# A metaformer with routed experts: tiles kept per half, expert buffers in the first half's memory, new instruction lists

## The chip, the cores and the metric

The kernel runs on one core of a Trainium2 chip. The time is that of the device, in microseconds, from the first to the last instruction of the program and a little around it; a figure for a kernel is the median of its runs. The core has five engines that work through lists of their own: TensorE (PE, with its weight loads shown apart as PEld), VectorE (DVE), ScalarE (ACT), GpSimd (POOL) and SyncE (SP, which issues most DMAs here). They wait for one another by semaphores.

## The reference

`x` holds 2 batches of 16 times by 64 patches, with 128 channels. It is normalised per position, goes through four layers of attention, and is added to its own input; then comes a layer of eight experts of which each token takes two.

```python
b, t, p, d = x.shape
for i in range(DEPTH):                                # 4 layers, 8 heads of 16
    xs = _layernorm(x.reshape(b * t, p, d), ln_s_g[i], ln_s_b[i])
    x_s = _attention(xs, w_qkv_s[i], w_out_s[i], b_out_s[i]).reshape(b, t, p, d)   # over 64 patches
    xt = (x + x_s).transpose(0, 2, 1, 3).reshape(b * p, t, d)
    xt = _layernorm(xt, ln_t_g[i], ln_t_b[i])
    x_t = _attention(xt, w_qkv_t[i], w_out_t[i], b_out_t[i])                       # over 16 times
    x_t = x_t.reshape(b, p, t, d).transpose(0, 2, 1, 3)
    x = _layernorm(x_s + x_t, ln_f_g[i], ln_f_b[i]) + x
```

```python
probs = jax.nn.softmax(xf @ Wr, axis=-1)
w, idx = jax.lax.top_k(probs, 2)
gates = jnp.zeros((n, e)).at[jnp.arange(n)[:, None], idx].add(w)
acc = acc + g[:, None] * (gelu(xf @ w1) @ w2)         # summed over the 8 experts, and added to x
```

## The kernel before

**Halves and units.** The two batches are the two halves of the work, 1024 tokens or 8 chunks of 128 each. A word such as `score.t10` names a step: `t` for temporal (`s` spatial, `e` the experts, `f` the layer's last norm), the half (1), and the group (0). Spatial attention of a half has two groups, temporal attention one unit. A minus behind the word means the layer before, a plus the next one.

**Steps of a layer.** DVE computes the moments (`stats`) and POOL the root (`stats` too, a power, line 499); DVE normalises four chunks and ACT the other four (`normal`); PE transposes them (`turn`). PE makes keys and queries (`project`, line 748) and values (`values`, line 727), DVE and POOL apply the rotation, and PE folds the keys' two parts into one (`fold`, lines 758 and 760). PE computes scores in two halves of four heads, `score` and `more` (line 795; temporal ones start from a mask, line 787). DVE takes the maximum off and ACT the exponential, first half `soft`, second half `rest`. PE transposes the probabilities (`head`, `tail`) and multiplies them with the values (`lead`, `mix`, line 832), DVE divides (`divide`), PE applies the output weights (`out`, line 868), and DVE adds the residual (`out`). `bias` and part of the last norm (`final`) prepare the next layer's sum. A matmul of float32 shows twice in the profile's counts.

**Glows.** A step `glow` is four matmuls of `ident` by `ident` into a bank of `turn` that no instruction reads (line 695).

**Experts.** For each half, PE computes the logits, DVE picks two experts per token (`rank`) and then the slot of each pair (`place`, which needs a small matmul of PE on `chosen`). POOL sends each token to its two slots by 16 indirect DMAs (`send`, line 540, two to a step), SP loads the slots back in four parts (line 468) once all 16 have landed, and DVE reads gates and owners from them (`origin`). Then 46 blocks of 128 slots are run: in tick i PE computes the first product of block i and the second of block i-1, DVE copies the first weights of block i+1 (`w1_now`, line 967) and scales the result of block i-1 (`y_sb`), and POOL sends that result back by an indirect DMA (line 549). At the end DVE adds the two answers to each token (`merge`).

**Order.** Each engine runs its steps strictly in order, and nothing but lists sets that order: `ORDERS` (line 102) for layers 0 to 2 and `TAIL` (line 130) for layer 3 and the experts, one list for each of PE, DVE, ACT and POOL. In `TAIL` the number behind `@` says ahead of which tick a step stands. Between them the list of PE in a layer reads, around the temporal score pairs of both halves:

```python
score.s11 more.s11 head.s10 lead.s10 tail.s10 mix.s10 score.t00 more.t00 head.s11 lead.s11 tail.s11 mix.s11 glow.s02 out.s10 glow.s07 glow.s01 glow.s03
head.t00 lead.t00 tail.t00 mix.t00 turn.t10 project.t10 out.t00 fold.t10 score.t10 more.t10 values.t10 glow.s04 turn.s00+ glow.s00
```

**Memory.** `x_res`, `x_bias`, `x_mid`, `x_sum` and `x_nrm` are one tile each for both halves. `qT`, `kE`, `v_s` and `prob` lie in an arena whose memory the experts' buffers (`slots0`, `slots1`, `xT`, `w1_now`, `hT`, `y_sb`) take over when attention is done with it.

## Time and profile before

| | us |
|---|---|
| median of three runs | 669.15 |
| lowest and highest run | 665.67, 670.98 |
| time of the profiled execution | 671.71 |
| its span in the trace | 669.9 |
| PE busy | 550.3 |
| DVE busy | 454.9 |
| ACT busy | 305.9 |
| POOL busy | 249.0 |

The profile covers one execution. Busy times count the instructions of an engine without its waits; a row of a timeline gives the start, the time, the engine, the line, the operation, what it writes and reads, how many instructions were merged into the row, and in brackets how long the engine had been idle and what released it. The granted clock of PE is given as a share of full speed: 1.00 is 2.4 GHz and 0.50 is 1.2 GHz.

### The profile page before, as it was taken

What the parts mean: (1) busy time and instruction counts of PE and PEld (TensorE: products, weight loads), DVE (VectorE), ACT (ScalarE), POOL (GpSimd) and SP (SyncE); (2) the same over time, 40 slices, a digit from 0 to 9 for tenths busy, and PEclk for the clock granted to TensorE, in tenths of its full rate; (3) what the DMA queues carried; (4) which work ended last, traced back from release to release, by engine and by line L of the source; (5) the groups of instructions that cost most, each with busy time, mean ns of one, the idle gap of its engine ahead of it and who ended that gap; (6) DMA issues with size and microseconds to landing.
All of it is one profiled execution on the core that took longest, in us unless ns stands there. A gap on an engine that the chain in (4) does not pass through costs nothing.

```text
span 669.9 us, 21398 instructions
## 1 busy us (share of the span) xinstructions
PE 550.3 (82%) x8984; PEld 432.4 (65%) x8984; DVE 454.9 (68%) x1336; ACT 305.9 (46%) x507; POOL 249.0 (37%) x197
## 2 busy tenths in 40 slices
PE   0978988897898977978988798889888736999991
PEld 0565676566756846665677467746766635999991
DVE  5586847948877576788755966986479676444444
ACT  1455833274466433744844256448434313343330
POOL 6403501441253031613700424154014273777642
PEclk9999979799999897989979979999798575999996
DMA  4000008400000100000001000000000014141314
GB/s 134 1 2 1 3 3 298 174 2 18 1 3 4 32 1 4 2 18 1 2 4 33 2 2 3 17 1 3 3 2 3 6 46 110 50 145 53 107 38 141
DMA packets 17425, 24.71 MB, mean 37 GB/s; under 512 B 2578, under 2 KB 12180, under 8 KB 17268
## 3 DMA queue, kind: packets, MB, share of 16 engines
q1 hardware_dynamic: 14836, 18.17, 8.7%
q0 software_dynamic: 2496, 5.18, 2.3%
q8 instruction: 73, 1.20, 0.8%
q14 instruction: 20, 0.16, 0.1%
...
## 4 chain that ended last, share of the span: by engine, by line
PE 63%; DVE 15%; ACT 11%; issue 5%; POOL 2%; DMA 2%; SPq 0%; DVEq 0%; ACTq 0%
PE turn L678 8%; PE small L832 8%; PE score L748 7%; PE score L795 7%; PE small L933 6%; PE score L921 6%; PE small L727 5%; PE turn L695 4%; PE turn L758 4%; PE turn L760 3%; DVE stats L955 3%; ACT probT L626 3%; PE small L868 3%; ACT prob L620 2%; ACT kE L613 2%
## 5 line engine op out<-in xcount | busy, mean ns | idle before, releaser
L499 POOL TENSOR_TENSOR rstd<-veps,mhalf 128x8 f32<-128x8 f32 x28 | 46.5, 1661 | 246.1 <-DVE veps L995 246.1
L626 ACT ACTIVATE probT<-turn 128x512 f32<-128x512 f32 x96 | 53.3, 597 | 94.9 <-PE turn L678 94.7
L1088 DVE TENSOR_REDUCE top<-score 128x16 f32<-128x1024 f32 (+1 forms) x48 | 58.5, 1219 | 39.2 <-PE score L795 39.2
L795 PE MATMUL score<-kE,qT 32*32 32x64 f32 (+1 forms) x3072 | 58.6, 261 | 12.2 <-issue 12.1
L795 PEld LDWEIGHTS score<-kE,qT 32*32 32x32 f32 (+1 forms) x3072 | 48.8, 123 | 27.1 <-issue 26.0
L678 PE MATMUL turn<-ident,prob 128*128 128x128 f32 x384 | 61.2, 311 | 2.9 <-ACT prob L620 2.9
L1090 DVE TENSOR_TENSOR prob<-score,top 128x1024 f32<-128x1024 f32 x48 | 58.8, 1224 | 1.6
L678 PEld LDWEIGHTS turn<-ident,prob 128*128 128x128 f32 x384 | 49.2, 160 | 6.7 <-ACT prob L620 3.6
L549 POOL DMA_INDIRECT answers<-y_sb,home x46 | 44.7, 971 | 23.9 <-DVE y_sb L1224 16.5
L832 PE MATMUL small<-v_s,probT 128*64 128x34 f32 x1024 | 43.0, 240 | 12.5 <-ACT probT L626 6.8
L620 ACT ACTIVATE prob<-prob 128x1024 f32<-128x1024 f32 x48 | 50.1, 1057 | 6.9 <-DVE prob L1090 6.7
L613 ACT ACTIVATE kE<-turn,hmask 128x512 f32<-128x512 f32 x64 | 39.9, 686 | 28.3 <-PE turn L760 28.1
L832 PEld LDWEIGHTS small<-v_s,probT 128*64 128x64 f32 x1024 | 39.0, 153 | 21.0 <-ACT probT L626 8.7
L921 PE MATMUL score<-xT,w_now 128*128 128x128 f32 x368 | 50.5, 282 | 1.2 <-ACT xT L657 0.9
L933 PE MATMUL small<-w_all,hT 128*128 x368 | 48.8, 276 | 0.0
L664 ACT ACTIVATE hT<-score 128x512 f32<-128x512 f32 x46 | 27.5, 597 | 46.1 <-PE score L921 46.1
L921 PEld LDWEIGHTS score<-xT,w_now 128*128 128x128 f32 x368 | 46.3, 198 | 2.0 <-issue 1.3
L604 ACT ACTIVATE v_t<-small 32x512 f32<-32x512 f32 x64 | 38.8, 607 | 17.2 <-PE small L727 16.5
L1058 DVE TENSOR_TENSOR rope<-score,cs_t 128x512 f32<-128x512 f32 x48 | 30.7, 681 | 23.5 <-PE score L748 23.5
L933 PEld LDWEIGHTS small<-w_all,hT 128*128 128x128 f32 x368 | 44.8, 192 | 0.2
L540 POOL DMA_INDIRECT dispatched<-routed,slot_idx x32 | 32.4, 1012 | 32.9 <-DVE slot_idx L1187 23.8
L695 PE MATMUL turn<-ident 128*128 128x128 f32 x280 | 40.0, 293 | 2.9 <-ACT xnT L589 1.5
...
## 6 DMA issues: line engine op xcount, KB each, us to landing
...
```

The lines of the kernel that those rows point to most:

```text
L613: last = nc.scalar.activation(kE[:, e, cols], turn[:, u % 2, :], ACT.Copy, scale=hmask[:, e:e + 1])
L620: nc.scalar.activation(p, p, ACT.Exp, scale=SCALE).then_inc(prob_ready, 1)
L626: nc.scalar.activation(probT[:, q.nth % 2, 2 * k:2 * k + 2, 2 * h:2 * h + 2, :].rearrange("p k g n -> p k (g n)"), turn[:, u % 2, :].rearr ...
L678: last = nc.tensor.transpose(turn[:, u % 2, j * P:(j + 1) * P], src, ident[:, :])
L695: nc.tensor.matmul(turn[:, q.turns % 2, 0:P], ident[:, :], ident[:, :], start=True, stop=True)
L748: nc.tensor.matmul(score[:, i % 4, :], w[:, off:off + P], cols, start=True, stop=True).then_inc(proj_full, 1)
L795: last = nc.tensor.matmul(score[b * n:(b + 1) * n, g, c * 2 * n:(c + 1) * 2 * n], qT[rows, tok:tok + n], kE[rows, :, tok:tok + n], start=q ...
L832: last = nc.tensor.matmul(cols[b * n:(b + 1) * n, :, g, :], probT[:, head.nth % 2, k, g, b * n:(b + 1) * n], v[:, blk0 + b, g, :], start=T ...
L921: last = nc.tensor.matmul(score[:, i % 4, c * P:(c + 1) * P], w1_now[:, i % WAYS, c * P:(c + 1) * P], xT[:, g % 2, b % XGROUP * P:(b % XGR ...
L933: last = nc.tensor.matmul(bank[:, 0:P], hT[:, j % 2, c * P:(c + 1) * P], w2_all[:, bass.ds(e, 1), c * P:(c + 1) * P].rearrange("p o n -> p ...
L1088: nc.vector.tensor_reduce(tops, mine, AX_X, ALU.max).then_inc(top_ready, 1)
L1090: nc.vector.tensor_tensor(prob[:, i % 2, 2 * h:2 * h + 2, :, :].rearrange("p g k (r n) -> p (g k r) n", n=block_len), mine, tops[:, :, Non ...
```

## The change

**Tiles.** `x_nrm`, `x_mid`, `x_bias`, `x_sum`, `x_res`, `qT` and `kE` become two tiles each, one for each half, all within the arena. `slots0`, `xT`, `w1_now` and `hT` move into what the first half's tiles held, `slots1` to the arena's start, `y_sb` into the memory of `kE` of the first half. All uses are rewritten to the half's own tile, with the same shapes.

**Lists.** All eight lists are new. On PE, steps are woven more finely: in a layer `tail.s10`, `head.s11` and `mix.s10` stand between `score.t00` and `more.t00`, and two glows between `score.t10` and `more.t10`; a layer has eight glows before and after, and the last layer with the ticks five instead of eleven. In `TAIL`, ticks 0 to 2 stand ahead of the second half's `place.e10` on PE and DVE, and the second half's sends are spread over ticks 1 to 8 on POOL. On DVE, `normal.e00` moves ahead of `rank.e00`, and `divide.s11` between `soft.t00` and `rest.t00`; on POOL, `stats.f10` stands behind six `send` steps of the first half instead of five.

```diff
-ARENA = (53760 + 16384) // 4
+HALF = 6 * HT * 4
+ARENA = (20480 + 2 * HALF + 16384 + 8704 + 16384 + 768) // 4
...
-        score.s11 more.s11 head.s10 lead.s10 tail.s10 mix.s10 score.t00 more.t00 head.s11 lead.s11 tail.s11 mix.s11 glow.s02 out.s10 glow.s07 glow.s01 glow.s03
+        score.s11 more.s11 head.s10 lead.s10 score.t00 tail.s10 head.s11 mix.s10 more.t00 tail.s11 lead.s11
...
-        origin.e00@0 place.e10@0 origin.e10@21 merge.e00@47 merge.e10@47
+        origin.e00@1 place.e10@3 origin.e10@24 merge.e00@47 merge.e10@47
...
-        qT = at("qT", [P, TOKENS], 20480)
-        kE = at("kE", [P, 2, TOKENS], 28672)
...
+        def halves(name, slot):
+            return [at(f"{name}{h}", [P, HC, P], 20480 + h * HALF + slot * HT * 4) for h in range(BATCH)]
+
+        x_nrm, x_mid, x_bias, x_sum, x_res = (halves(name, i) for i, name in enumerate(("x_nrm", "x_mid", "x_bias", "x_sum", "x_res")))
+        qT = [at(f"qT{h}", [P, HT], 20480 + h * HALF + 5 * HT * 4) for h in range(BATCH)]
+        keys = 20480 + 2 * HALF
+        kE = [at(f"kE{h}", [P, 2, HT], keys + h * 8192) for h in range(BATCH)]
...
-        hT = at("hT", [P, 2, FF], 24576)
-        slots1 = at("slots1", [P, BLOCKS, ROW], 28672)
-        y_sb = at("y_sb", [P, ANSWERS, P], 17664)
-        w1_now = at("w1_now", [P, WAYS, FF], 40832)
...
+        slots0 = at("slots0", [P, BLOCKS, ROW], 20480)
+        xT = at("xT", [P, 2, XGROUP * P], 20480 + 12160)
+        w1_now = at("w1_now", [P, WAYS, FF], 20480 + 12160 + 4096)
+        hT = at("hT", [P, 2, FF], 20480 + 12160 + 8192)
+        y_sb = at("y_sb", [P, ANSWERS, P], keys)
+        slots1 = at("slots1", [P, BLOCKS, ROW], 0)
```

**PE, from the first half's temporal scores to out.s10, in a layer.** Before, the two score halves (each a mask and 64 matmuls on `kE` and `qT`) stand together, and glows (`turn<-ident`) around `out.s10` (`o_nrm` and the 128x128 matmuls on `xnT`):

```order
L787 MATMUL score<-pmask 128x512 x2
L795 MATMUL score<-kE,qT 32x64 x64
L787 MATMUL score<-pmask 128x512 x2
L795 MATMUL score<-kE,qT 32x64 x64
L678 MATMUL turn<-ident,prob 128x128 x8
L832 MATMUL small<-v_s,probT 64x34 x16
L678 MATMUL turn<-ident,prob 128x128 x8
L832 MATMUL small<-v_s,probT 64x34 x16
L695 MATMUL turn<-ident 128x128 x4
L678 MATMUL turn<-ident,o_nrm 128x128 x8
L868 MATMUL small<-ws,xnT 128x128 x8
L695 MATMUL turn<-ident 128x128 x12
```

In the changed kernel the same place reads:

```order
L791 MATMUL score<-pmask 128x512 x2
L799 MATMUL score<-kE_64,qT_62 32x64 x64
L685 MATMUL turn<-ident,prob 128x128 x16
L836 MATMUL small<-v_s,probT 64x34 x16
L791 MATMUL score<-pmask 128x512 x2
L799 MATMUL score<-kE_64,qT_62 32x64 x64
L685 MATMUL turn<-ident,prob 128x128 x8
L836 MATMUL small<-v_s,probT 64x34 x32
L685 MATMUL turn<-ident,o_nrm 128x128 x8
L872 MATMUL small<-ws,xnT 128x128 x8
L685 MATMUL turn<-ident,prob 128x128 x16
L702 MATMUL turn<-ident 128x128 x8
```

Sixteen transposes and 16 matmuls on `probT` have moved between the two score halves, no glow stands next to `out.s10`, and two glows (8 matmuls) stand behind the transposes of `head.t00` and `tail.t00`.

**PE, the second half's temporal scores, in a layer.** Before, the folds, the two score halves, the values, a glow, and the next layer's `turn.s00` between two glows:

```order
L758 MATMUL turn<-rope_49,ident 128x512
L760 MATMUL turn<-rope_50,exch 128x512
L787 MATMUL score<-pmask 128x512 x2
L795 MATMUL score<-kE,qT 32x64 x64
L787 MATMUL score<-pmask 128x512 x2
L795 MATMUL score<-kE,qT 32x64 x64
L727 MATMUL small<-wt,xnT 32x64 x64
L695 MATMUL turn<-ident 128x128 x4
L678 MATMUL turn<-ident,x_nrm 128x128 x8
L695 MATMUL turn<-ident 128x128 x4
```

In the changed kernel:

```order
L731 MATMUL small<-wt,xnT 32x64 x64
L762 MATMUL turn<-rope_49,ident 128x512
L764 MATMUL turn<-rope_50,exch 128x512
L762 MATMUL turn<-rope_49,ident 128x512
L764 MATMUL turn<-rope_50,exch 128x512
L791 MATMUL score<-pmask 128x512 x2
L799 MATMUL score<-kE_65,qT_63 32x64 x64
L702 MATMUL turn<-ident 128x128 x8
L791 MATMUL score<-pmask 128x512 x2
L799 MATMUL score<-kE_65,qT_63 32x64 x64
L685 MATMUL turn<-ident,x_nrm_52 128x128 x8
```

The values have moved ahead of the folds, and two glows stand between the score halves and none behind them.

**DVE, the second half's `place.e10` and the first blocks.** Before, the end of `place.e10` (down to `code_of`) stands ahead of the copies of tick 1 and 2 (a load of the expert's number, then `w_now<-w_all`) and of the scaling of block 0 (`y_sb`):

```order
L1191 TENSOR_TENSOR reach<-small_60,rc 128x184
L1193 TENSOR_REDUCE picked<-reach 128x23
L1194 TENSOR_SCALAR expert_of<-picked 128x23
L1196 TENSOR_SCALAR code_of<-picked 128x23
L966 TENSOR_LOAD expert_of
L966 ISA x2
L967 ISA
L967 COPY w_now<-w_all 128x512
L1224 TENSOR_SCALAR y_sb<-small,gate 128x128
L966 TENSOR_LOAD expert_of
```

In the changed kernel the end of `origin.e00` (`home`), ticks 1 and 2, and then the start of `place.e10`:

```order
L1210 SCALAR_TENSOR_TENSOR home<-slots_78,picked 128x23
L970 TENSOR_LOAD expert_of
L970 ISA x2
L971 ISA
L971 COPY w_now<-w_all 128x512
L1223 TENSOR_SCALAR y_sb<-small,gate 128x128
L970 TENSOR_LOAD expert_of
L970 ISA x2
L971 ISA
L971 COPY w_now<-w_all 128x512
L1223 TENSOR_SCALAR y_sb<-small,gate 128x128
L1171 TENSOR_SCALAR small_68<-small 128x8
```

Two copies and two scalings, those for blocks 2 and 3 and of blocks 0 and 1, now stand ahead of `place.e10`.

## Rows read from the trace of the kernel before

**Rows 1.** The page, busy time: us, share of the span, instructions of one engine.

```profile
PE 550.3 (82%) x8984; PEld 432.4 (65%) x8984; DVE 454.9 (68%) x1336; ACT 305.9 (46%) x507; POOL 249.0 (37%) x197
```

**Rows 2.** The page, the chain that ended last: shares of the span by engine.

```profile
PE 63%; DVE 15%; ACT 11%; issue 5%; POOL 2%; DMA 2%; SPq 0%; DVEq 0%; ACTq 0%
```

**Rows 3.** Stages: stretch, length, busy (instructions) of PE, PEld, DVE, ACT, POOL; PE's granted clock; DMA.

```profile
148.30:275.50 127.20, 109.49 (x2028) 81.23 (x2024) 94.14 (x262) 65.57 (x109) 39.83 (x28) 0.93 0.03 8
...
511.50:558.90 47.40, 30.62 (x520) 26.50 (x516) 33.07 (x130) 13.57 (x24) 23.84 (x20) 0.65 0.08 25
571.40:656.40 85.00, 84.76 (x750) 84.12 (x750) 35.50 (x93) 32.58 (x55) 57.25 (x59) 1.00 0.25 79
```

**Rows 4.** Stages: six stretches at half clock (two, sum), one more, one at full clock.

```profile
214.80:221.60 6.80, 5.77 (x138) 4.96 (x133) 4.01 (x4) 2.14 (x3) 0.00 (x0) 0.50 0.01 2
255.80:262.50 6.70, 5.67 (x239) 4.90 (x237) 6.56 (x20) 1.65 (x4) 1.64 (x1) 0.50 0.02 5
...
sum 47.30, PE 41.12 PEld 34.32 DVE 33.58 ACT 12.88 POOL 4.91; mean PE 6.85 PEld 5.72 DVE 5.60 ACT 2.15 POOL 0.82
...
474.20:481.00 6.80, 6.61 (x117) 5.70 (x99) 2.73 (x3) 2.74 (x4) 0.00 (x0) 0.50 0.02 5
351.40:381.90 30.50, 25.02 (x367) 18.64 (x363) 22.31 (x81) 10.97 (x20) 8.39 (x6) 1.00 0.06 19
```

**Rows 5.** Timeline of PE around out.s10, layer 1: start, us, instructions, [idle before].

```profile
228.15 2.84 PE L695 MATMUL turn<-ident 128*128 128x128 f32 x24
...
232.38 0.86 PE L832 MATMUL small<-v_t,probT 128*32 128x68 f32 x32 [0.52 <-DVE x_sum L1002]
...
237.13 1.09 PE L678 MATMUL turn<-ident,x_nrm 128*128 128x128 f32 x8
```

**Rows 6.** Timeline of PE, layer 1, from more.t00 on.

```profile
216.50 1.11 PE L795 MATMUL score<-kE,qT 32*32 32x64 f32 x57 [1.03 <-issue]
...
219.44 1.95 PE L832 MATMUL small<-v_s,probT 128*64 128x34 f32 x32
...
222.78 1.17 PE L832 MATMUL small<-v_s,probT 128*64 128x34 f32 x32 [0.25 <-ACT probT L626]
```

**Rows 7.** Timeline of PE, layer 1: values.t00, then values.t10.

```profile
191.91 1.99 PE L727 MATMUL small<-wt,xnT 128*32 128x64 f32 x128
...
259.57 3.51 PE L727 MATMUL small<-wt,xnT 128*32 128x64 f32 x128
```

**Rows 8.** Timeline of DVE, layer 1: out.s10's first sum, normal.t10's products.

```profile
227.56 0.69 DVE L1116 TENSOR_TENSOR x_mid<-small,x_bias 128x512 f32<-128x512 f32 x1 [2.71 <-PE small L868]
...
233.38 1.11 DVE L1024 TENSOR_SCALAR x_nrm<-x_mid,mv,rstd 128x128 f32<-128x128 f32 x4
```

**Rows 9.** Timeline of PE, start of layer 2: lead.s00.

```profile
291.95 0.67 PE L832 MATMUL small<-v_s,probT 128*64 128x34 f32 x16 [1.47 <-DVE x_sum L1125]
```

**Rows 10.** Timeline of DVE: the first instruction of rank.e00.

```profile
524.33 0.22 DVE L1139 TENSOR_TENSOR marks<-small,rstd 128x64 f32<-128x64 f32 x1 [3.01 <-PE small L878]
```

**Rows 11.** Timeline of DVE: normal.e10's products; the weight copy for block 2.

```profile
563.75 1.11 DVE L1024 TENSOR_SCALAR routed<-x_in,mv,rstd 128x128 f32<-128x128 f32 x4
...
570.88 0.43 DVE L967 COPY w_now<-w_all 128x512 f32 x1 [0.76 <-DVE code_of L1196]
```

**Rows 12.** Timeline of POOL: the tenth send of the first half, then stats.f10.

```profile
545.06 0.96 POOL L540 DMA_INDIRECT dispatched<-routed,slot_idx  x1 [0.30 <-issue]
546.98 1.70 POOL L499 TENSOR_TENSOR rstd<-veps,mhalf 128x8 f32<-128x8 f32 x1 [0.96 <-DVE veps L995]
```

**Rows 13.** Timeline of PE: place.e10, block 4, the second half's first slots.

```profile
563.81 0.23 PE L887 MATMUL small<-chosen,tri 128*128 128x64 bf16 x1 [5.03 <-DVE chosen L1162]
...
575.12 1.06 PE L921 MATMUL score<-xT,w_now 128*128 128x128 f32 x8
...
607.37 0.60 PE L678 MATMUL turn<-ident,slots 128*128 128x128 f32 x4
```

**Rows 14.** Loads of the slots (line 468): from issue to landing.

```profile
DMA to landing us min/median/max: 3.3/5.2/6.9
```

150 lines of the change are left out of this document (69 added, 81 removed).

## The prediction

> **What bounds the kernel now.** I read the page's busy lines first, then the chain that ended last, then the busy times by stage, and only then single instructions. PE is busy for 82% of the span [rows 1]. The chain runs through PE for 63% and through DVE for 15% [rows 2], so PE's list decides, and DVE's where PE waits. By stage [rows 3]: layer 1, which stands for the three full layers, takes 127.2 us with PE busy 109.49 at a granted clock of 0.93; the stretch in which the two halves are routed takes 47.4 with PE busy only 30.62 at 0.65; the expert blocks take 85.0 with PE busy 84.76 at 1.00. In the blocks only PE's own speed counts. What new lists can change lies in the layers and in the 47.4 us of routing.
>
> Two things cost PE time in a layer. The first is the clock. In each of layers 0 to 2 there are two longer stretches at a granted 0.50, which is 1.2 GHz of 2.4: six in all, 47.3 us with PE busy 41.12, and a seventh in layer 3 of 6.8 with 6.61 busy [rows 4]. In each case PE had just run a pair of temporal score halves. In layer 1, score.t00 and more.t00 stand back to back, 128 matmuls each in the profile's count, and the clock falls at 214.8, within the second; behind score.t10 and more.t10 it falls at 255.8 [rows 4]. The second thing is the glows, matmuls of ident by ident that nobody reads: of the four that stand around out.s10 in PE's list, the three behind it take 2.84 us [rows 5].
>
> **The change part by part.** *Tiles per half and the arena.* The same instructions work on the same shapes; only addresses differ. I put that at nothing, and both bounds too: no row shows an operation that would change.
>
> *The clock at score pairs.* The new list puts tail.s10, head.s11 and mix.s10 between score.t00 and more.t00, and two glows between score.t10 and more.t10; in layer 3 the t00 pair is split too (by tail.s10 and mix.s10), the t10 pair is not. What a half-clock stretch costs: 32 narrow matmuls take 1.95 against 1.17 [rows 6], 128 value matmuls 3.51 against 1.99 [rows 7]. By the last pair the factor is 1.76, so the six stretches lose 41.12 x (1 - 1/1.76) = 17.8 and the seventh 6.61 x 0.432 = 2.9: together 20.6, some 2.9 each. PE is late all through these stretches, so nothing hides it. The bounds are 0 (the clock falls all the same) and 20.6 (it never does). The nearest row for a split pair is the stretch from 351.4 to 381.9, which kept 1.00 with PE busy 25.02 of 30.5 [rows 4]; the nearest against it is that in a pair PE has also an idle time of 1.03 that a split does not take away [rows 6]. Halfway between them I take half, 10.3.
>
> The Trainium skill, page "TensorE: Matmul & The Clock Gate", section "Part 4: PE-mode transpose", says that the full rate does not engage for transposes, which are not counted as busy in the same way. By that rule transposes between the two halves of a pair would hold nothing, and this term would be nearer 0. Here the trace speaks against it in part: from 219.44 to 222.78 PE ran only narrow matmuls and transposes, and the clock came back between them [rows 6].
>
> *The glows.* There are eight per layer before and after. Of the four around out.s10, one goes from ahead of out.s10 and three from ahead of head.t00; two stand now behind tail.t00, where PE would wait for x_sum anyway (0.52 before [rows 5]). What that gives is capped by DVE, which is late next: from out.s10's first sum at 227.56 to the end of normal.t10's products at 234.49 [rows 8], so turn.t10 could start at 234.5 where it starts at 237.13 [rows 5]: 2.6 at most. Against it stands a new wait: divide.s11 now stands between soft.t00 and rest.t00 on DVE, and out.s10 waits for what follows it. I take 2.0 per layer, bounds 0 and 2.6, over four layers 8.0. The other glows go into waits as they did. values.t10 moves from behind more.t10 to ahead of fold.t10: its 1.99 [rows 7] leaves one place of PE's path and enters another, nothing.
>
> *The start of a layer.* head.s01 and tail.s00 now fill the 1.47 that lead.s00 waits for x_sum [rows 9]; but lead.s01 then waits for divide.s00, which stands behind stats.f10 on DVE. Bounds 0 and 1.5 for each of three layers; nearer to nothing, since the wait is only moved, and I take nothing.
>
> *Routing of the first half.* normal.e00 moves ahead of rank.e00 on DVE, into 3.01 us in which DVE waits for the logits [rows 10]; its 1.1, by the 1.11 of normal.e10 [rows 11], leaves the path to the first send. But stats.f10's pow now stands behind 12 sends instead of 10, at 0.96 and 0.30 between two of them, 1.26 each, and DVE's final.f10 waits for it: before, POOL had been free for 0.96 when it was wanted [rows 12], so 2.5 - 0.96 = 1.5 comes back. Sum 0.4 lost; bounds 1.1 gained (the pow is hidden) and 1.5 lost. I take nothing.
>
> *Blocks ahead of the second half's routing.* PE waits 5.03 for chosen before place.e10 [rows 13]; blocks 0 to 2 now stand ahead of that. Yet blocks 2 and on need weight copies from DVE, and DVE works in order. Before, it begins normal.e10's products at 563.75, then does origin.e00 and place.e10 up to 570.12 (the copy for block 2 at 570.88, less the 0.76 ahead of it [rows 11]): 6.4. From there to PE's matmuls of block 4 at 575.12 [rows 13] it does three copies and two y_sb: 5.0. After, the same 6.4 + 5.0 stand between 563.75 and block 4, in another order: two copies and two y_sb between origin.e00 and place.e10. So PE's wait only moves, from ahead of block 0 to ahead of block 4. Bounds: 5.0 gained (the whole wait of PE) and 0.8 lost (one more such wait of 0.76 for PE's place.e10). I take nothing.
>
> *Second half's sends.* They begin when place.e10's indices stand, one copy (0.43 + 0.76) ahead of block 4's start after, so at some 574, and seven answers of the first blocks stand between them on POOL: 16 + 7 = 23 transfers of 1.26 [rows 12] are 29, so the last goes at 603 and the slots land 5.2 later [rows 14], at 608. PE wants the second half's first slots at 607.37 [rows 13], and a shift of all that went before moves both. Bounds 0 and 2 lost; I take nothing, since origin.e10 has been put three blocks later as well.
>
> **The sum.** 10.3 + 8.0 = 18.3. The profiled execution's span is 669.9 and its own time 671.71, so 1.8 lies around the span; 669.9 - 18.3 + 1.8 = 653.4. That execution was 2.6 above the median of the three runs, 669.15: I forecast 651 as a median.
>
> **The rivals.**
> 1. *The clock holds at all seven pairs.* For it: most of what PE did just ahead of each fall was the pair itself. Against: the 1.03 of idle time within the pair stays [rows 6]. 669.15 - 20.6 - 8.0 = 640.6.
> 2. *The clock falls as often.* For it: only transposes and narrow matmuls stand between the t00 halves. 669.15 - 8.0 = 661.2. This is also what the rule on transposes in the Trainium skill, named above, would make of t00.
> 3. *The glows were needed.* Without four of them between mix.s11 and mix.t00, PE runs only transposes and narrow matmuls there, and a new stretch at 0.50 appears in each of four layers: 4 x 2.9 = 11.6 is given back. 651 + 11.6 = 662.6.
> 4. *Slower.* From more.s11 to out.s10's full matmuls the new list has nothing but narrow matmuls and transposes: four sets of 8 transposes at 1.09 [rows 5], four of 32 narrow matmuls at 1.17 and two score halves of 128 x 1.11 / 57 / 1.76 = 1.4 [rows 6], some 12 us at full clock. If the clock stays at 0.50 there to the end, that costs 12 x 0.76 = 9.1 instead of 2.9, 25 more in four layers; less the 8.0 of glows the time is 669 + 17 = 686. It decides against the change when more than some 6.5 us of that work runs at half clock.
> 5. *The blocks do fill the wait.* DVE turns out not to bind, and blocks 0 to 2 fill the 5.03 of PE's wait [rows 13]: 5 more, 646.
>
> **How the numbers follow.** My forecast 0.37; rival 1 0.18; rival 2 0.20; rival 3 0.12; rival 4 0.08; rival 5 0.05. 1% is 6.7 us, about what a measurement of this kernel can tell from no change. Faster by over 1% (below 662.5): 0.37 + 0.18 + 0.05 + half of rival 2's and a little of rival 3's = 0.72. Slower: 0.09. The rest, 0.19, is within 1%. The range for 8 in 10 reaches from just below rival 1 to rival 2 with its own error: 638 to 667. The forecast's own range, with the clock terms between 6 and 15 and the glows between 0 and 10, is 644 to 663.
>
> **What would show it.** Clock: in the stage table of the new kernel, the stretches at 0.50 behind score.t00 or score.t10 should be about half as many as seven; every one kept costs 2.9. Glows: turn.t10 should wait for x_nrm of DVE, some 7 us behind out.s10's first sum. Blocks: PE should wait some 2 to 3 us for w_now ahead of block 4. Sends: a wait for the second half's slots of at most 2 us. The prediction is wrong if the layers do not shorten by some 4 to 6 us each, or if the stretch from the last score pair to block 4 changes by more than 3 us.

## The result: no change, at 669.33 us

The changed kernel took 669.33 us as a median of 20 runs (657.13 to 678.70), the kernel before 670.01 as a median of 20 (665.67 to 672.75). The forecast was 651, in a range of 638 to 667. The ratio that the comparison gives is 0.9909 (95% interval 0.9883 to 0.9935), but it leaves out every run more than 1.5% above its kernel's fastest, and the new kernel scatters so widely that this was more than half of its runs; medians over all runs are compared here, and by them nothing changed. The clock did not change either: the mean granted clock of an execution is 0.914 as a median of the 20 runs, and 0.917 over the 123 runs of the kernel before that stand beside the experiments. The profiled execution took 674.03, 4.7 above the median; its span is 672.1.

The page's busy time and chain of the changed kernel answer to [rows 1] and [rows 2]:

```profile
PE 556.5 (83%) x8936; PEld 433.6 (65%) x8936; DVE 454.9 (68%) x1336; ACT 307.3 (46%) x507; POOL 249.2 (37%) x197
...
PE 59%; DVE 21%; ACT 7%; issue 6%; POOL 4%; DMA 1%; DVEq 0%; SPq 0%; ACTq 0%; POOLq 0%
```

PE has 48 instructions less (six glows) and is busy 6.2 us longer: it ran more of its work at half clock. The chain goes through DVE for more of the span (21% against 15%). The stages, to be read beside [rows 3] (layer 1; the routing of both halves, with values.t10 in it now; the blocks, here from block 4 on, in [rows 3] from block 2 on):

```profile
152.30:281.40 129.10, 112.88 (x2028) 82.72 (x2024) 94.30 (x262) 65.92 (x109) 39.97 (x28) 0.92 0.03 8
512.90:561.10 48.20, 30.92 (x628) 26.91 (x628) 34.64 (x135) 14.41 (x25) 21.72 (x20) 0.65 0.11 34
576.40:658.70 82.30, 81.93 (x726) 81.25 (x726) 33.89 (x89) 30.92 (x52) 57.76 (x59) 1.00 0.26 82
```

Layer 1 is 1.9 longer in this execution, the routing 0.8 longer, and PE is still busy without a break in the blocks. The stretches at half clock that follow a temporal pair in layers 0 to 3 of this execution, beside [rows 4]:

```profile
86.70:100.30 13.60, 13.22 (x238) 10.94 (x239) 3.72 (x6) 5.25 (x8) 0.00 (x0) 0.50 0.01 2
131.10:144.70 13.60, 13.43 (x287) 10.11 (x287) 8.44 (x25) 5.38 (x10) 1.64 (x1) 0.50 0.02 5
216.40:219.80 3.40, 3.40 (x16) 2.85 (x15) 0.00 (x0) 2.20 (x4) 0.00 (x0) 0.50 0.02 5
260.80:274.40 13.60, 13.06 (x176) 9.06 (x176) 7.45 (x13) 6.54 (x12) 0.00 (x0) 0.50 0.01 2
387.10:400.70 13.60, 12.72 (x198) 9.14 (x198) 7.13 (x11) 5.82 (x10) 0.00 (x0) 0.50 0.01 2
472.40:486.00 13.60, 13.60 (x357) 11.69 (x337) 4.30 (x8) 4.28 (x6) 0.00 (x0) 0.50 0.02 4
sum 71.40, PE 69.44 PEld 53.79 DVE 31.04 ACT 29.47 POOL 1.64; mean PE 11.57 PEld 8.97 DVE 5.17 ACT 4.91 POOL 0.27
```

Before, seven stretches held 41.12 + 6.61 = 47.7 us of PE's work; now six hold 69.4. One pair kept the clock (layer 2's first), one lost it only shortly (layer 1's first), and the other five have stretches of 13.6. All three second pairs of layers 0 to 2 are among these. PE's timeline of the one in layer 0:

```profile
131.09 2.04 PE L799 MATMUL score<-kE,qT 32*32 32x64 f32 x128
133.07 3.78 PE L702 MATMUL turn<-ident 128*128 128x128 f32 x16
136.78 1.03 PE L791 MATMUL score<-pmask 2*128 2x512 bf16 x2
137.74 2.04 PE L799 MATMUL score<-kE,qT 32*32 32x64 f32 x128
139.72 1.97 PE L685 MATMUL turn<-ident,x_nrm 128*128 128x128 f32 x8
141.85 4.66 PE L752 MATMUL score<-xnT,ws 128*128 128x512 f32 x7 [0.17 <-ACT xnT L596]
```

The two glows between the halves take 3.78 us at half clock and do not bring it back; more.t10, turn.s00 and most of project.s00 run at half clock behind them. In this execution the split stretched the time at half clock instead of ending it. That is not the lists alone: in the kept execution of `e5_old_tail` (below), whose lists of layers 0 to 2 are the same, two of the three stretches behind the second pairs are short:

```profile
129.00:139.20 10.20, 9.54 (x151) 6.67 (x151) 5.23 (x10) 4.95 (x9) 0.79 (x1) 0.50 0.01 3
255.30:258.70 3.40, 3.40 (x31) 3.23 (x31) 2.83 (x5) 0.28 (x1) 0.00 (x0) 0.50 0.02 5
378.20:381.60 3.40, 3.40 (x52) 3.23 (x52) 2.56 (x4) 0.00 (x0) 0.00 (x0) 0.50 0.02 5
```

### The profile page after: what moved, and what is told of

It reads as the page before. It is cut to its first block, busy times and chain, and to the rows that moved or that the text cites. A ratio compares the mean times of both kernels' runs of the same rounds, so it can differ in the third digit from the quotient of the medians.

```text
span 672.1 us, 21303 instructions
## 1 busy us (share of the span) xinstructions
PE 556.5 (83%) x8936; PEld 433.6 (65%) x8936; DVE 454.9 (68%) x1336; ACT 307.3 (46%) x507; POOL 249.2 (37%) x197
## 4 chain that ended last, share of the span: by engine, by line
PE 59%; DVE 21%; ACT 7%; issue 6%; POOL 4%; DMA 1%; DVEq 0%; SPq 0%; ACTq 0%; POOLq 0%
PE turn L685 9%; PE score L799 7%; PE score L752 6%; PE small L937 6%; PE small L836 6%; PE score L925 6%; DVE stats L959 5%; PE turn L762 4%; PE turn L764 4%; PE small L731 4%; PE turn L702 3%; PE small L872 3%; POOL rstd L507 2%; ACT xnT L647 2%; DVE mv L990 2%
## 5 line engine op out<-in xcount | busy, mean ns | idle before, releaser
L799 PE MATMUL score<-kE,qT 32*32 32x64 f32 (+1 forms) x3072 | 62.9, 267 | 9.0 <-issue 8.5
L799 PEld LDWEIGHTS score<-kE,qT 32*32 32x32 f32 (+1 forms) x3072 | 51.7, 125 | 26.3 <-issue 22.5
L557 POOL DMA_INDIRECT answers<-y_sb,home x46 | 45.1, 980 | 20.6 <-DVE y_sb L1223 11.7
L1103 DVE RECIPROCAL den<-small 128x16 f32<-128x16 f32 x64 | 16.1, 252 | 48.8 <-PE small L836 48.3
L836 PE MATMUL small<-v_s,probT 128*64 128x34 f32 x1024 | 40.7, 240 | 6.9 <-DVE o_nrm L1105 4.2
L647 ACT ACTIVATE xnT<-turn 128x512 f32<-128x512 f32 x32 | 17.4, 594 | 58.5 <-PE turn L685 58.5
L518 POOL TENSOR_TENSOR rope<-rope,cs_s 128x512 f32<-128x512 f32 x16 | 20.3, 1270 | 62.3 <-DVE rope L1078 62.3
```

Source lines behind the costliest of these rows:

```text
L557: nc.gpsimd.indirect_dma_start(ys[h], bass.IndirectOffsetOnAxis(home[:, h, b % BLOCKS:b % BLOCKS + 1].bitcast(U32), 0), y_sb[:, b % ANSWER ...
L799: last = nc.tensor.matmul(score[b * n:(b + 1) * n, g, c * 2 * n:(c + 1) * 2 * n], qT[q.half][rows, tok:tok + n], kE[q.half][rows, :, tok:t ...
L836: last = nc.tensor.matmul(cols[b * n:(b + 1) * n, :, g, :], probT[:, head.nth % 2, k, g, b * n:(b + 1) * n], v[:, blk0 + b, g, :], start=T ...
```

## The experiments

Eighteen kernels ran in batches, each batch beside runs of the kernel before. The difference is between medians of one batch; 6 to 12 runs of each kernel stand behind a median, and their spread is mostly 5 to 12 us (19 in f4, 15 in j2, and one run of e5 took 804.99), so that two medians less than some 2 us apart are not told apart. Two kernels of different batches are compared by their differences to the kernel before; four medians stand behind such a figure, and below some 4 us it is not told from chance by itself. If the recorded runs are drawn again at random, 95 of 100 draws put f1 between 4.0 and 12.0 behind e5, but f3 anywhere from 6.8 ahead of e5 to 0.5 behind it. The last two columns give the mean granted clock, as the median over the same runs: it tells whether a difference in time is one of the clock. Ratios come with a 95% interval and leave out runs as said above.

| run | what it is | median | before beside it | difference | clock | clock before |
|---|---|---|---|---|---|---|
| (the change) | all of it | 669.33 | 670.01 | -0.7 | 0.914 | 0.917 |
| e6_tiles_only | new tiles, old lists | 669.37 | 668.66 | +0.7 | 0.915 | 0.917 |
| e4_old_layers | new list of layer 3 and experts alone | 672.70 | 668.66 | +4.0 | 0.906 | 0.917 |
| e5_old_tail | new lists of layers 0 to 2 alone | 665.35 | 668.66 | -3.3 | 0.927 | 0.917 |
| e1_join_both | the change, all split pairs joined again | 672.94 | 668.66 | +4.3 | 0.916 | 0.917 |
| f1_t00_joined | e5, first pair joined | 673.34 | 668.76 | +4.6 | 0.911 | 0.917 |
| f2_values_between | e5, values between the second pair | 665.55 | 668.76 | -3.2 | 0.926 | 0.917 |
| f3_glows_at_out | e5, glows at out.s10 | 663.03 | 668.76 | -5.7 | 0.930 | 0.917 |
| f4_tail_joined | the change, first pair joined in layer 3 | 669.84 | 668.76 | +1.1 | 0.920 | 0.917 |
| h1_t10_as_before | e5, second pair as before | 663.52 | 669.37 | -5.9 | 0.926 | 0.916 |
| h2_tail_glows | the change, six glows in layer 3 | 664.14 | 669.37 | -5.2 | 0.933 | 0.916 |
| h3_glows_in_waits | f3, two glows more per layer | 663.40 | 669.37 | -6.0 | 0.930 | 0.916 |
| h4_both | h2 and the glows of f3 | 662.04 | 669.37 | -7.3 | 0.932 | 0.916 |
| j1_glows_old_t10 | h4, second pair as before | 659.47 | 669.05 | -9.6 | 0.929 | 0.918 |
| j2_first_three | the change, three glows in layer 3 | 663.95 | 669.05 | -5.1 | 0.925 | 0.918 |
| j3_old_split_t00 | the kernel before, first pair split | 670.65 | 669.05 | +1.6 | 0.914 | 0.918 |
| j4_all_glows | j1, two glows more per layer | 653.70 | 669.05 | -15.4 | 0.940 | 0.918 |
| k1_old_lists_glows | the kernel before, four glows per layer | 668.56 | 669.59 | -1.0 | 0.925 | 0.914 |
| k2_all_glows_t00_joined | j4, first pair joined | 659.00 | 669.59 | -10.6 | 0.931 | 0.914 |

### Which part of the change does what

All edits are to the changed kernel where nothing else is said. The pairs joined again:

```diff
-        score.s11 more.s11 head.s10 lead.s10 score.t00 tail.s10 head.s11 mix.s10 more.t00 tail.s11 lead.s11
+        score.s11 more.s11 head.s10 lead.s10 tail.s10 head.s11 mix.s10 score.t00 more.t00 tail.s11 lead.s11
...
-        values.t10 fold.t10 score.t10 glow.s07 glow.s06 more.t10 turn.s00+ project.s00+ fold.s00+ values.s00+
+        values.t10 fold.t10 score.t10 more.t10 glow.s07 glow.s06 turn.s00+ project.s00+ fold.s00+ values.s00+
...
-        score.t00@0 tail.s10@0 mix.s10@0 more.t00@0 tail.s11@0 lead.s11@0 mix.s11@0 out.s10@0 glow.s00@0
+        tail.s10@0 mix.s10@0 score.t00@0 more.t00@0 tail.s11@0 lead.s11@0 mix.s11@0 out.s10@0 glow.s00@0
```

> The changed kernel, but with both temporal score pairs put back together in every layer: score.t00 directly ahead of more.t00 (tail.s10, head.s11 and mix.s10 go ahead of the pair) and score.t10 directly ahead of more.t10 (the two glows go behind it). In the changed kernel's trace the granted clock stays at 0.50 for 13.6 us behind score.t10 in each of layers 0 to 2 and for 13.6 to 17 us at score.t00 in layers 0 and 3, where before it was 6.8 to 10.2. Theory A (the clock does not come back as long as temporal scores are still being computed, so a split pair makes one longer stretch): these stretches shrink to 6.8 to 10, PE's work at half clock in layers 0 to 3 goes from 76.9 us towards the 46.6 of before, at 0.43 us each some 10 to 13 us: about 657 to 660. Theory B (the clock is lost for want of the glows around out.s10 and of the values behind the second pair): nothing comes back, 668 to 672. Theory C (the split did help and something else eats the gain): slower, 673 to 680.

It took 672.94, with a ratio to the kernel before of 1.0068 (1.0033 to 1.0104). Nothing came back, so theory A, which the first trace of the change had suggested, does not hold for the pairs together. The time lies between the ranges of theories B and C; C comes nearer with what follows: some split helps, and something else eats the gain.

Old lists in layers 0 to 2 (of PE, shown here, and of the other engines):

```diff
 ORDERS = {
     "PE": """
-        score.s00 glow.s00 head.t10- more.s00 lead.t10- tail.t10- mix.t10- score.s01 head.s00 more.s01 out.t10-
...
+        score.s00 more.s00 glow.s06 head.t10- lead.t10- tail.t10- mix.t10- head.s00 score.s01 more.s01 out.t10- lead.s00 tail.s00 mix.s00 head.s01 lead.s01 tail.s01 mix.s01 glow.s05
...
```

> The new tiles and the new list of the last layer and the experts, with the lists of layers 0 to 2 as they were before. Theory A (the new lists of the layers lose at the clock what they gain in waits): layers 0 to 2 take again 117.8, 127.2 and 130.5 us, and the last layer keeps its gain of six glows, 5.5 us less its longer stretch at half clock: 665 to 668 with little scatter between runs. A rival (the layers' lists carry the gain, the last layer's lose it): 670 to 675.

The old lists in the last layer and the experts, again of all engines:

```diff
 TAIL = {
     "PE": """
-        score.s00@0 head.t10-@0 more.s00@0 lead.t10-@0 tail.t10-@0 score.s01@0 mix.t10-@0 more.s01@0 out.t10-@0
...
+        head.t10-@0 score.s00@0 more.s00@0 glow.s12@0 lead.t10-@0 tail.t10-@0 mix.t10-@0 score.s01@0 more.s01@0 out.t10-@0 head.s00@0 lead.s00@0 tail.s00@0 mix.s00@0 head.s01@0
...
```

> The new tiles and the new lists of layers 0 to 2, with the list of the last layer and the experts as it was before (eleven glows in it, place.e10 ahead of all blocks). Theory A: the layers' lists alone give about no change, 668 to 674, with a scatter of some 3% between runs as in the changed kernel; the eleven glows cost the last layer some 5 us against the changed kernel. The rival (the layers' lists carry the gain): 660 to 665.

Both edits at once leave the new tiles alone:

> The new tiles and addresses alone, with all lists as before. The prediction's step that tiles and the arena cost nothing: 668 to 672, stage for stage the times of before within 1 us. The rival (the new addresses make accesses collide, or the one tile per half changes which instruction waits): 3 us or more to either side, to be seen in the mean time of an instruction of DVE, ACT or POOL on x_res, x_sum, qT or kE.

The tiles do nothing: 1.0020 (0.9991 to 1.0048). The new lists of the layers gain 3.3 (0.9941, 0.9910 to 0.9972), the new list of the last layer loses 4.0 (1.0048, 1.0016 to 1.0080), and together they about cancel, as in the change. The clock goes with both: 0.927 and 0.906, against 0.917 beside them. That is the rivals' side of both expectations: the last layer's list, with six glows fewer, is the one that loses.

### The first pair

> The new tiles, the new lists of layers 0 to 2 and the old list of the last layer (the kernel that took 665.35 as a median), with score.t00 and more.t00 put back together in layers 0 to 2; score.t10 and more.t10 stay apart with two glows between. Both pairs joined had cost 3.6 us against the changed kernel (672.94 against 669.33). Theory D (the split at t00 keeps the clock): the loss comes back here, 668 to 670. Theory E (the glows between the halves of t10 keep the clock, the split at t00 does nothing or lengthens its stretch): 663 to 666.

The edit is the first piece of the diff above, on the new layers with the old last layer. It took 673.34, 4.6 above the kernel before where e5 was 3.3 below it: the split of the first pair is worth 7.9 us in layers 0 to 2, or 2.6 in each if they share alike. That is theory D, by more than it expected, and it is the clock: 0.927 with the split and 0.911 without. In the kept executions (e5's is its fastest run, f1's is at its median) the stretches at 0.50 behind the first pairs of layers 0, 1 and 2 are 6.8, 6.8 and 3.4 us without the split; with it there is one of 3.4, in layer 1. The stage of layer 1 from score.t00 to out.s10, with the split (e5) and then without it (f1), in the columns of the stages above:

```profile
207.60:221.60 14.00, 12.19 (x384) 9.82 (x380) 6.90 (x13) 6.33 (x10) 0.00 (x0) 0.88 0.01 2
```

```profile
214.40:226.20 11.80, 9.50 (x334) 7.80 (x333) 4.75 (x10) 2.31 (x4) 0.00 (x0) 0.71 0.02 4
```

The split stage holds 16 transposes and 32 narrow matmuls more (as the profile counts them) and still runs at a mean clock of 0.88 against 0.71. In the old lists, though, the same split brings nothing:

```diff
-        score.s11 more.s11 head.s10 lead.s10 tail.s10 mix.s10 score.t00 more.t00 head.s11 lead.s11 tail.s11 mix.s11 glow.s02 out.s10 glow.s07 glow.s01 glow.s03
+        score.s11 more.s11 head.s10 lead.s10 score.t00 tail.s10 mix.s10 more.t00 head.s11 lead.s11 tail.s11 mix.s11 glow.s02 out.s10 glow.s07 glow.s01 glow.s03
```

> The kernel before (about 669), with one edit in the list of layers 0 to 2: score.t00 goes ahead of tail.s10 and mix.s10, so that these two stand between the halves of the first pair. All else is as before. The prediction's clock step (a split pair keeps the clock in half of the cases, 2.9 us each): three pairs in layers 0 to 2, 4 to 8 us less, 661 to 665. The rival (the split helps only together with the rest of the new lists): 667 to 671.

It took 670.65, a ratio of 1.0011 (0.9979 to 1.0044), at a clock of 0.914 against 0.918. There only tail.s10 and mix.s10 stand between the halves, without head.s11. In the last layer, where the change also puts only these two between them, the split was undone (the last piece of the diff above):

> The changed kernel with score.t00 and more.t00 put back together in the last layer alone (behind tail.s10 and mix.s10). With the old lists in layers 0 to 2, the last layer's new list took 115.85 us to the end of its last scores where the old one took 111.16, with 32.9 us against 5.3 at half clock, though it has six glows fewer. Theory F (the split pair in the last layer keeps the clock down): the stretch at half clock from score.t00 to out.s10 falls from 17 to 24 us to 7 to 10, and the time falls by some 4 to 5: 664 to 666. Theory G (the clock is down there for want of the glows at score.s11, out.s10 and head.t00): no change, 668 to 671.

It took 669.84, 1.1 above the kernel before where the change is 0.7 below. Its runs reach from 659.00 to 678.15, so a gain or loss of 2.6 by this one pair would not show, and what the split does in the last layer is not known. The 664 to 666 of theory F is not what was measured, so theory G was left: the missing glows.

### The glows

> The same base (665.35), with three glows around out.s10 in layers 0 to 2 again (one ahead of it, two behind it; one fewer behind tail.t00). The prediction's rival 3 (the glows were needed there for the clock): the half-clock time at the first pair shrinks, and the time falls to 658 to 662. The prediction's own step (a glow there only delays turn.t10): 2 us per layer come back, 669 to 672. If neither the clock nor the path to turn.t10 is moved by them: 664 to 667.

```diff
-        mix.s11 out.s10 head.t00 tail.t00 glow.s05 glow.s04 lead.t00 turn.t10 mix.t00 project.t10 out.t00
+        mix.s11 glow.s10 out.s10 glow.s11 glow.s12 head.t00 tail.t00 glow.s05 lead.t00 turn.t10 mix.t00 project.t10 out.t00
```

It took 663.03, between the ranges of rival 3 and of no effect, and 5.7 below the kernel before where e5 is 3.3 below: 2.4 gained, which is not told from chance, with the clock at 0.930 against 0.927. What the run does exclude is the prediction's 2 us of loss per layer. PE's timeline of layer 1 says why the glows cost nothing. Without them (e5), from the end of mix.s11 to turn.t10 and project.t10:

```profile
218.17 2.48 PE L835 MATMUL small<-v_s,probT 128*64 128x34 f32 x64
221.66 1.06 PE L684 MATMUL turn<-ident,o_nrm 128*128 128x128 f32 x8 [1.01 <-DVE o_nrm L1104]
...
231.25 1.31 PE L684 MATMUL turn<-ident,x_nrm 128*128 128x128 f32 x8 [1.00 <-DVE x_nrm L1024]
```

With them (f3):

```profile
221.79 1.53 PE L835 MATMUL small<-v_s,probT 128*64 128x34 f32 x44 [0.65 <-issue]
223.25 1.16 PE L701 MATMUL turn<-ident 128*128 128x128 f32 x8
224.33 1.06 PE L684 MATMUL turn<-ident,o_nrm 128*128 128x128 f32 x8
...
227.53 1.95 PE L701 MATMUL turn<-ident 128*128 128x128 f32 x16
...
233.94 1.31 PE L684 MATMUL turn<-ident,x_nrm 128*128 128x128 f32 x8
```

From mix.s11's end to turn.t10 it is 231.25 - 220.65 = 10.6 without and 233.94 - 223.32 = 10.6 with: two glows more fill the waits of 1.01 for o_nrm and of 1.00 for x_nrm, and DVE sets the distance either way.

In the last layer, six glows at waits of PE:

```diff
-        score.s10@0 more.s10@0 fold.t00@0 values.s10@0 score.s11@0 head.s10@0 more.s11@0 lead.s10@0 head.s11@0
-        score.t00@0 tail.s10@0 mix.s10@0 more.t00@0 tail.s11@0 lead.s11@0 mix.s11@0 out.s10@0 glow.s00@0
-        head.t00@0 tail.t00@0 lead.t00@0 mix.t00@0 turn.t10@0 project.t10@0 out.t00@0 fold.t10@0 score.t10@0
-        more.t10@0 turn.e00@0 logits.e00@0 values.t10@0 place.e00@0 head.t10@0 lead.t10@0 tail.t10@0 mix.t10@0
+        score.s10@0 more.s10@0 fold.t00@0 values.s10@0 score.s11@0 head.s10@0 more.s11@0 lead.s10@0 glow.s20@0 head.s11@0 score.t00@0 tail.s10@0 mix.s10@0 more.t00@0 tail.s11@0 lead.s11@0 mix.s11@0 glow.s21@0 out.s10@0 glow.s00@0 glow.s22@0
+        head.t00@0 tail.t00@0 glow.s23@0 lead.t00@0 mix.t00@0 turn.t10@0 project.t10@0 out.t00@0 fold.t10@0 glow.s24@0 score.t10@0
+        more.t10@0 turn.e00@0 logits.e00@0 values.t10@0 glow.s25@0 place.e00@0 head.t10@0 lead.t10@0 tail.t10@0 mix.t10@0
```

> The changed kernel (669.33) with six glows more in the last layer, at places where PE waits: ahead of head.s11, ahead of out.s10 and behind it, ahead of lead.t00, ahead of score.t10 and ahead of place.e00. Theory G (the new list of the last layer loses 3 to 4 us because glows are missing): 664 to 667, and the last layer's time at half clock falls below 10 us. The rival (glows are pure cost, or the loss lies in the blocks): 670 to 674.

It took 664.14, 5.2 below the kernel before (0.9933, 0.9900 to 0.9965) where the change is 0.7 below: 4.5 gained, with the clock at 0.933 against 0.914. Theory G holds. PE's timeline of the changed kernel at the last layer's first pair:

```profile
470.52 1.09 PE L685 MATMUL turn<-ident,prob 128*128 128x128 f32 x8 [1.13 <-ACT prob L627]
...
472.08 1.92 PE L799 MATMUL score<-kE,qT 32*32 32x64 f32 x128
473.93 1.97 PE L685 MATMUL turn<-ident,prob 128*128 128x128 f32 x8
475.83 1.95 PE L836 MATMUL small<-v_s,probT 128*64 128x34 f32 x32
```

And with the six glows (h2), the same place:

```profile
460.24 1.16 PE L701 MATMUL turn<-ident 128*128 128x128 f32 x8
461.44 1.09 PE L684 MATMUL turn<-ident,prob 128*128 128x128 f32 x8
...
463.00 1.48 PE L798 MATMUL score<-kE,qT 32*32 32x64 f32 x128
464.41 1.09 PE L684 MATMUL turn<-ident,prob 128*128 128x128 f32 x8
465.75 1.17 PE L835 MATMUL small<-v_s,probT 128*64 128x34 f32 x32 [0.25 <-ACT probT L632]
```

The stage of h2 from score.t00 to out.s10, in the columns of the stages above:

```profile
462.40:473.80 11.40, 10.31 (x383) 8.60 (x381) 5.00 (x11) 4.88 (x8) 0.00 (x0) 1.00 0.02 4
```

PE waits 1.13 for prob ahead of head.s11 in the change, and the clock falls within the scores that follow; with a glow in that wait the clock stays at 1.00, and the transposes and narrow matmuls between the halves run in 1.09 and 1.17 instead of 1.97 and 1.95. Which of the six does it, the three near the pair (glow.s20, glow.s21 and glow.s22) or the other three:

> The changed kernel (669.33) with only three of the six glows in the last layer: ahead of head.s11, ahead of out.s10 and behind it (all six took 664.14). If the glows near the first pair hold the clock there: 664 to 666, the last layer without a fall of the clock from score.t00 to out.s10. If the other three, ahead of lead.t00, score.t10 and place.e00, do it: 668 to 670.

It took 663.95, 5.1 below the kernel before: the three near the pair are enough, as far as six runs between 660.93 and 675.92 tell. The kept execution, though it took 668.99, holds the clock at this place, from ahead of score.t00 to out.s10:

```profile
468.20:481.00 12.80, 12.01 (x395) 10.05 (x394) 6.90 (x12) 5.98 (x10) 0.00 (x0) 1.00 0.02 4
```

So do all six kept executions with a glow ahead of the last layer's head.s11 (h2, h4, j1, j2, j4, k2). In the four with the last layer's new list and no glow there (the change, e1, e4, f4) the clock falls between head.s11 and out.s10.

More glows in layers 0 to 2, at the waits ahead of lead.s01 and score.t10, on top of f3:

```diff
-        head.s01 tail.s00 lead.s00 mix.s00 lead.s01 tail.s01 mix.s01 glow.s01 glow.s02 out.s00 turn.s10
+        head.s01 tail.s00 lead.s00 mix.s00 glow.s13 lead.s01 tail.s01 mix.s01 glow.s01 glow.s02 out.s00 turn.s10
...
-        values.t10 fold.t10 score.t10 glow.s07 glow.s06 more.t10 turn.s00+ project.s00+ fold.s00+ values.s00+
+        values.t10 fold.t10 glow.s14 score.t10 glow.s07 glow.s06 more.t10 turn.s00+ project.s00+ fold.s00+ values.s00+
```

> The version with three glows at out.s10 in layers 0 to 2 and the old list of the last layer (663.03), with two glows more in each of these layers, at the waits of 1.81 us ahead of lead.s01 and of 1.55 us ahead of score.t10. Theory I (every glow that fills a wait of PE costs no time and makes falls of the clock rarer): 658 to 661. The rival (the clock falls at the temporal scores whatever stands ahead of them, and the gain of the glows at out.s10 was that of another stage): 662 to 665.

No change (663.40), as the rival had it. The glows of f3 and h2 together:

> The changed kernel with both: three glows around out.s10 in layers 0 to 2 and the six glows in the last layer. If theory G and the gain of 2.3 us of the first three add up: 662 to 665. If the last layer's new list loses its time elsewhere (in the blocks): 666 to 669.

It took 662.04, 2.1 below h2, as a sum would have it; by itself that is not told from chance, and the clock is the same (0.932 against 0.933). And the kernel before, with four glows at its own waits (ahead of lead.s00, turn.t00, project.t10 and score.t10):

```diff
-        score.s00 more.s00 glow.s06 head.t10- lead.t10- tail.t10- mix.t10- head.s00 score.s01 more.s01 out.t10- lead.s00 tail.s00 mix.s00 head.s01 lead.s01 tail.s01 mix.s01 glow.s05
+        score.s00 more.s00 glow.s06 head.t10- lead.t10- tail.t10- mix.t10- head.s00 score.s01 more.s01 out.t10- glow.s10 lead.s00 tail.s00 mix.s00 head.s01 lead.s01 tail.s01 mix.s01 glow.s05
...
```

> The kernel before (about 669) with four glows more in layers 0 to 2, at its own waits: ahead of lead.s00 (1.47 us), of turn.t00 (1.09), of project.t10 (1.41) and of score.t10 (1.71). If glows in waits are what was missing in both kernels: 660 to 664. If the new lists are needed for it: 667 to 671.

It took 668.56, a ratio of 0.9978 (0.9949 to 1.0008): glows alone do not help the old lists. They do raise the clock there, to 0.925 from 0.914, and the time does not follow, so they cost PE about as much elsewhere; where was not looked at.

### The second pair, and a faster version

> The same base (665.35), with values.t10 between score.t10 and more.t10 in place of the two glows, which go behind more.t10. Theory E in its general form (dense work between the halves of the second pair brings the clock back ahead of more.t10): the values do it as the glows did and are work that has to be done anyway, so the time is 662 to 666. A rival (only glows, which are full 128 by 128 matmuls, bring it back, and values of 32 columns do not): as with the joined pair, 668 to 671.

```diff
-        values.t10 fold.t10 score.t10 glow.s07 glow.s06 more.t10 turn.s00+ project.s00+ fold.s00+ values.s00+
+        fold.t10 score.t10 values.t10 more.t10 glow.s07 glow.s06 turn.s00+ project.s00+ fold.s00+ values.s00+
```

665.55, the same as with glows between (665.35). It does not tell whether either of them helps. The second pair as it was before the change does better than both:

```diff
-        values.t10 fold.t10 score.t10 glow.s07 glow.s06 more.t10 turn.s00+ project.s00+ fold.s00+ values.s00+
+        fold.t10 score.t10 more.t10 values.t10 glow.s07 turn.s00+ glow.s06 project.s00+ fold.s00+ values.s00+
```

> The new tiles, the new lists of layers 0 to 2 and the old list of the last layer (665.35 as a median), with the second pair as it was before the change: score.t10, more.t10, then values.t10, then two glows on either side of turn.s00. With the first pair joined this base took 673.34, 4 us more than the old lists, so something in the new lists loses time. Theory H (it is the second pair: its glows end ahead of more.t10, and the values no longer run behind it while the clock comes back): 659 to 662. The rival (the second pair's order does not matter, as with the values between its halves, 665.55): 664 to 667.

663.52 (six runs), 5.9 below the kernel before against 3.3, a gain of 2.6. On top of h4 the same edit gave 659.47, 9.6 below against 7.3, a gain of 2.3:

> The changed kernel with three glows around out.s10 in layers 0 to 2, six more glows in the last layer (both together took 662.04), and the second pair as before the change: score.t10, more.t10, values.t10, a glow, turn.s00, a glow. On the base without these glows the second pair's old order measured 663.52 against 665.35. If that adds up: 659 to 661. If the second pair's order does not matter: 661 to 664.

Each of the two is within what chance can give; both go the same way. The clock is not what they gain: it is 0.926 with the old order and 0.927 with the new one (h1 and e5), 0.929 and 0.932 on top of the glows (j1 and h4). And two glows more per layer, at the waits ahead of lead.s01 and score.t10, on top of that:

> As j1_glows_old_t10, with two glows more in layers 0 to 2, at the waits ahead of lead.s01 and of score.t10. If every glow in a wait makes falls rarer: 656 to 659. As measured on another base (no change from these two, 663.40 against 663.03): the time of j1_glows_old_t10 within 1 us.

653.70 (652.39 to 658.87), a ratio to the kernel before of 0.9782 (0.9740 to 0.9825): faster than both kernels, and the fastest here. The two glows that did nothing in h3 gave 5.8 us here, and the clock rose from 0.929 to 0.940. The page of its fastest run, PE's timeline there at layer 2's second pair, and layer 1 as in [rows 3]:

```profile
PE 550.3 (85%) x9080; PEld 434.4 (67%) x9080; DVE 453.8 (70%) x1336; ACT 306.4 (47%) x507; POOL 248.8 (38%) x197
```

```profile
366.27 1.05 PE L701 MATMUL turn<-ident 128*128 128x128 f32 x8
367.99 0.59 PE L790 MATMUL score<-pmask 2*128 2x512 bf16 x2 [0.66 <-ACT kE L619]
```

```profile
147.10:269.00 121.90, 110.03 (x2060) 82.34 (x2056) 94.03 (x262) 65.71 (x109) 39.77 (x28) 0.97 0.03 9
```

It has 144 instructions of PE more than the change and 6.2 us less of busy time; a glow fills most of the wait for kE that was 1.55, and layer 1 takes 121.9 at a mean clock of 0.97. Last, the split of the first pair undone in it:

> The version that took 653.7, with score.t00 and more.t00 put back together in layers 0 to 2 (the last layer's pair stays split). If the split works by itself, 2.7 us per layer as measured without the glows: 660 to 662. If the glows at out.s10 and the split do the same thing: 653 to 656.

659.00, 10.6 below the kernel before against 15.4, at a clock of 0.931 against 0.940: the split is still worth 4.8 beside the glows.

## Why the prediction was wrong

**What bounds the kernel: right.** PE's list decides; apart from e4 and e5, which exchange the lists of all engines, every experiment that moved the time moved only PE's steps.

**Tiles and arena: right**, nothing (e6).

**The two terms that made up the sum are the steps that failed**: 10.3 for the clock at the score pairs and 8.0 for the glows, 18.3 together, of which 0.7 was measured.

**The clock at the pairs: failed.** The term let half of the work at half clock go. Over all runs nothing of it went: 0.914 against 0.917; in the profiled execution PE's work at half clock behind the pairs rose from 47.7 to 69.4, which at the prediction's own price of 0.432 is 9.4 us lost. The price was right. Between the change's fastest run (657.13 at 0.937) and its slowest (678.70 at 0.899) lie some 54 us at half clock (an estimate: twice the time, times what the clock lacks to 1) and 21.6 us, 0.40 for each; the prediction had 20.6 for 54.1, or 0.38. What was wrong is how the clock would go. The split of the first pair does hold it in three layers (7.9 us by f1, 2.6 each and nearly the whole 2.9; 4.8 by k2, 1.6 each and about the half that was taken). But the term counted each split by itself, and the rest of the new lists lowers the clock: with the first pair joined they run at 0.911, below the 0.917 of the kernel before, and take 4.6 longer (f1), and the new list of the last layer alone runs at 0.906 and takes 4.0 longer (e4). In the old lists the split gave nothing (j3), and in the last layer its effect is not known (f4). That head.s11 between the halves is the reason was not tried by itself.

**The second pair: no gain from the split.** Putting the old order back gave 2.6 (h1) and 2.3 (j1), each within chance and neither in the clock. In the changed kernel's trace a reason can be read: with the clock once down, the glows between the halves and more.t10 behind them all run at half clock, 13.6 us at a stretch, where values.t10 behind a joined pair had ended it after 6.7 in layer 1 [rows 4]. But e5's execution of the same order had 10.2, 3.4 and 3.4, so this reason is not shown, and what the second pair costs, if it costs anything, is open.

**The glows: failed.** The sum counted 8.0 us gained for glows taken from PE's list. The trace of before showed the waits around them, but the argument took the distance from out.s10 to turn.t10 as theirs. Measured, glows put into the waits of the new lists gained 4.5 in the last layer (h2), by the clock, and 2.1 to 2.4 in layers 0 to 2 (h4 against h2, f3 against e5), which is not told from nothing: leaving them out gained no time anywhere. There was a gain on that path in layer 1, of the size forecast, but another edit made it. In the kernel before, mix.s11 ends at 222.78 + 1.17 = 223.95 [rows 6] and turn.t10 begins at 237.13 [rows 5], 13.2 behind it; in the new lists turn.t10 begins 10.6 behind it with the glows as well as without, 2.6 less, because mix.t00 now stands behind turn.t10 instead of ahead of it. In the last layer mix.t00 has stayed ahead of turn.t10, so the term's fourth layer had nothing to stand on. Why these 2.6 us a layer do not show in the kernel's time is open.

**The rivals.** Rival 3 comes nearest in kind: the glows were needed for the clock in the last layer. But the fall stands within score.t00 (from 472.4), not between mix.s11 and mix.t00 where rival 3 put it, and the glow that holds the clock stands ahead of head.s11, in front of the pair. Rival 2 (the clock falls as often) without its 8.0 for glows comes out at the 669 that was measured, and the clock over all runs is nearly what it was, but gains and losses that it does not name make up that number. The mechanism of rival 4 showed at the first pairs of layers 0 and 3 in the profiled execution (13.6 each), though not its size.

**The rule on transposes** in the Trainium skill (page "TensorE: Matmul & The Clock Gate", section "Part 4: PE-mode transpose") is not borne out for the float32 transposes of this kernel. In layer 1 of the change PE ran nothing but transposes from 216.40 to 219.80 (the third row of the half-clock stretches above: 16 instructions, busy 3.40), and the clock was back at once behind them:

```profile
219.80:223.20 3.40, 3.40 (x167) 2.74 (x166) 2.47 (x6) 0.91 (x2) 0.00 (x0) 1.00 0.00 0
```

**Start of a layer**: the new wait stood where it was forecast, ahead of lead.s01 (1.81 us, the wait that h3 and j4 fill), here in layer 2 of the change; its price was not measured by itself:

```profile
303.12 1.13 PE L836 MATMUL small<-v_s,probT 128*64 128x34 f32 x32 [1.81 <-DVE o_nrm L1105]
```

**Routing of the first half: the loss right, the gain not.** In the changed kernel's timelines of POOL and DVE, final.f10 waits for the later power (549.62 + 1.67 = 551.29):

```profile
549.62 1.67 POOL L507 TENSOR_TENSOR rstd<-veps,mhalf 128x8 f32<-128x8 f32 x1
```

```profile
551.38 2.19 DVE L1040 SCALAR_TENSOR_TENSOR x_res<-x_nrm,rstd,x_bias 128x128 f32<-128x128 f32 x8 [1.83 <-issue]
```

The wait is 1.83 where 1.5 was forecast. The 1.1 of normal.e00 did not come back. The end of more.t10 on PE and the first send on POOL, before and then in the change:

```profile
516.71 1.40 PE L795 MATMUL score<-kE,qT 32*32 32x64 f32 x81 [1.33 <-issue]
533.45 1.18 POOL L540 DMA_INDIRECT dispatched<-routed,slot_idx  x1 [12.86 <-DVE slot_idx L1187]
```

```profile
517.95 0.90 PE L799 MATMUL score<-kE,qT 32*32 32x64 f32 x41 [1.37 <-issue]
534.35 1.18 POOL L548 DMA_INDIRECT dispatched<-routed,slot_idx  x1 [13.03 <-DVE slot_idx L1186]
```

The send goes 533.45 - 518.11 = 15.3 behind more.t10 before and 534.35 - 518.85 = 15.5 after. Behind `chosen`, where normal.e00 had stood, DVE now waits 0.86 for PE's place.e00:

```profile
531.12 0.17 DVE L1171 TENSOR_SCALAR small<-small 128x8 f32<-128x8 f32 x1 [0.86 <-PE small L896]
```

**Blocks ahead of the routing: right.** In the changed kernel's timeline of PE, the wait stands ahead of block 4:

```profile
576.47 1.13 PE L925 MATMUL score<-xT,w_now 128*128 128x128 f32 x8 [2.94 <-issue]
```

Forecast was 2 to 3 us for w_now. The profile puts the wait down to issue, but DVE's copy for block 4 ends 0.1 ahead of it, at 575.94 + 0.43 = 576.37:

```profile
575.94 0.43 DVE L971 COPY w_now<-w_all 128x512 f32 x1 [0.77 <-DVE code_of L1195]
```

From the end of more.t10 to block 4 it is 576.47 - 518.85 = 57.6 where it was 575.12 - 518.11 = 57.0. Rival 5 fell.

**Sends: right.** No wait for the second half's slots is in PE's waits from 576 on.

**Together**: in the new lists the split of the first pair gains 7.9. Against it stand the 4.5 of the last layer's missing glows, and, each within chance, the glows of layers 0 to 2 (2.1 to 2.4) and the order of the second pair (some 2.4). That is about all of it, but these figures come from kernels that differ in more than one edit; they are no exact sum.
